# Routing in three batches of six tiles and one of seven, expert 0 split by ScalarE and VectorE, the gates' store before the expert loads

## The chip, the core and the metric

The program runs on one core of a Trainium2 chip. The metric is the device time of one execution in microseconds (us), lower is better. TensorE (PE) multiplies matrices out of SBUF into PSUM banks; VectorE (DVE), ScalarE (ACT) and GpSimd (POOL) work element by element; SyncE (SP) and the others issue transfers (DMA). Every engine runs its own list of instructions in order and waits for the others by semaphores.

## What is computed

A graph layer over 3125 nodes of 256 features and 53125 edges, sorted by the node they end at, and then a mixture of eight experts, of which each node uses its best two:

```python
h   = layernorm(x);  z = h @ W_func.T
e   = leaky_relu(concat(z[src], z[dst], edge_attr) @ W_att.T)
alpha = softmax of e over the edges of one dst
x   = x + h + relu(where(deg > 0, h @ W_self.T + segment_sum(alpha * z[src], dst), h))
t   = layernorm(x)                          # rows for the router and the experts
probs = softmax(t @ router_w.T);  top 2 of 8, renormalised -> gates
y_e = (silu(t @ w1[e].T) * (t @ w3[e].T)) @ w2[e].T
out = x + sum over e of gates[e] * y_e
```

## The kernel before

**The stream.** The nodes are 25 tiles of 128 rows (`TILES`); the edges are 104 groups of 512 (`GROUPS`). For each group POOL gathers four times 128 rows of z (`gather`, L826), DVE and ACT make the scores, their running maximum and the weights, PE multiplies them with the rows (`weighted`, L1347), and DVE adds the sums of two groups to `acc` (`add_sums`, L1869). `run` writes this as a software pipeline: in each turn a stage with lag n works on the group of n turns ago. The turns are 0 to 103 for group t's first stages, and go on until the stage with the largest lag is through. Stages passed through `tiled` work once in four turns on a node tile whose edges are complete: its denominator (`den_of`, L1581 to L1585), its share (ACT), a transpose and two products on PE (`node_parts`), the residual and second norm on DVE and ACT, the transpose and router product on PE (`hn2_T`, `logits_of`), and at the end `logit_copy` (L1626) with lag 34.

**Routing.** A batch of tiles (`ROUTES`) is routed on DVE once its logits are there: `first_choice`, `second_choice` (with the running counts `prefix`, L1673), `ranks_of` after two small products on PE (`rank_of`), `gates_of` (L1683 to L1690), and then pairs of one-hot rows for three tile and choice pairs at a time (`one_hots`, L1716 and L1717), which PE multiplies (`tokens_of`, L1277). The first three batches run in the stream, one step a turn behind the turn's other work; the last one after it, with the step that makes the list of slots (`slot_rows`, L1747) and of the expert of each slot.

**The experts.** There are 56 slots of 128 rows. Each expert's weights (`W`, 2.1 MB) are split into a high part (ACT copies it into the matrix type, L542) and a low part (the rest, a subtraction by `split_lo`, L551), in two pieces of 2842 and 1422 columns. Expert 0 is split by POOL alone (`split_first`, L558 and L563) once the stream's last product is done. Expert 1 is split by ACT and POOL while slot 0 runs (`second_hi`, `second_expert`). For the others ACT makes the high part, DVE the first low piece and POOL the second, in the turns after the expert's predecessor begins (`at_new_expert`). POOL gathers the rows of a slot (L876), PE transposes them, ACT and DVE make high and low rows (L1111, L1984), PE makes the first 384 hidden columns (`up_first`, L1411) and then the rest, ACT and DVE the gated hidden rows (L1118, L1970), PE transposes those (L1440), ACT and DVE split them (L1124, L1993, L1996), PE multiplies (L1450 for the high, L1457 for the low part), DVE weighs the result (`gated`, L2008, L2011) and POOL adds it into the output by an indirect transfer (L869).

**SP.** After the stream SP issues the loads of experts 1 and 2 (L696), then the gates' two stores (L770 for 20 tiles, L772 for 5), and then tells POOL that the first part is over. POOL's first gather of rows waits for both stores and for `slot_rows`. ACT's `second_hi` waits in turn 1 for expert 1's load, ahead of slot 0's first activation.

Of the kernel before, what the change touches and what calls it, by code (L numbers as in the profile page):

```python
# [30 lines left out]
P = 128  # L31
N, C, EDGES, EF = 3125, 256, 53125, 64
# [56 lines left out]
ROUTE_RING = 2  # L89
CHUNK = 3  # L90
# [13 lines left out]
def build(nc, x, src, src_batch, dst, dst_by_edge, dst_ends, mark_rows, wt, w_func, w_func_t, w_self_t, att_nodes, att_edge,  # L104
# [7 lines left out]
    with ExitStack() as ctx:  # L112
# [38 lines left out]
        split_next = sb("split_next", [1, SLOTS], i32)  # L151
# [4 lines left out]
        rt = sb("rt", [P, 4 * RB * E + 4 * RB * E + 5 * RB + (RB + 1) * E + 12 * RB + CELLS + TILES + 2 * E + 6 * E + 2  # L156
# [43 lines left out]
        iota_h, o = carve(ef, o, [2 * P], fp16)  # L200
        assert o <= 5 * WE
# [82 lines left out]
        gates, o = carve(rt, o, [TILES, E])  # L284
# [22 lines left out]
        split_f, o = carve(acc, o, [SLOTS])  # L307
        behind_f, o = carve(acc, o, [SLOTS])
        dump_p, o = carve(acc, o, [1])
# [96 lines left out]
        first_hi = sem("first_hi")  # L406
# [147 lines left out]
        def split_first(pool):  # L554
            pool.wait_ge(experts_in[0], 16)
            for piece in range(2):
                a, b = PIECES[piece]
                nc.gpsimd.tensor_tensor(split(0, 0, piece), raw(0, piece), ones[:, 0:1].to_broadcast([P, b - a]), ALU.mult)\  # L558
                    .then_inc(first_hi, 1)
            for piece in range(2):  # L560
                pool.wait_ge(first_hi, 1 + piece)
                pool.sem_inc(hi_split, 1)
                nc.gpsimd.tensor_tensor(split(0, 1, piece), raw(0, piece), split(0, 0, piece).bitcast(fp32), ALU.subtract)\  # L563
                    .then_inc(lo_split[piece], 1)

# [11 lines left out]
        def early_route(t):  # L577

            for b, (lo, hi) in enumerate(ROUTES[:-1]):
                i = t - BATCH * (hi - 1)  # L580
                if 0 <= i < 5 + CHUNKS_OF[b]:
                    return b, i
            return None, None

        def at_new_expert(eng, t, work):


            if isinstance(t, int) and t == 0:
                return
            e = eng.value_load(split_next[0:1, bass.ds(t, 1)], min_val=0, max_val=E - 1)  # L590
            with eng.If(e > 0):
                eng.wait_ge(y_psum, t)
# [1477 lines left out]
```

## Time and profile before

| | |
|---|---|
| median of 3 runs | 1061.29 us (1060.54 to 1061.91) |
| profiled execution | 1062.78 us, of which the span from first to last instruction is 1061.0 us |
| PE busy | 845.9 us (80%) |
| DVE busy | 648.2 us (61%) |
| POOL busy | 591.3 us (56%) |
| ACT busy | 449.6 us (42%) |
| last gather of the stream issued | 576.3 us |
| last product of the stream ends | about 604.7 us |
| routing of the last batch begins | 646.39 us |
| first expert product | 670.00 us |

The profiled execution is 1.49 us above the median of the runs, and 1.78 us of it lie outside the span. Times in the text are us from the start of the span. The program has three parts: up to 604.7 us the stream, up to 670 us a stretch of small dependent steps, and from there the 56 slots, in which PE is nearly always busy.

### The profile page before, as it was taken

The page shows a single profiled execution, that of the slowest core. Times are in us where ns is not written, and L with a number is a line of the kernel's source. Part 1 is how long each engine was busy: PE and PEld are TensorE (multiplying, and loading weights), DVE is VectorE, ACT ScalarE, POOL GpSimd, SP SyncE. Part 2 cuts the span into 40 slices and gives each one's busy share as a digit, 9 for nine tenths or more (in the row PEclk, how much of TensorE's full clock was granted, in tenths as well). Part 3 has the DMA queues.
Part 4 walks back from the last instruction along what each step waited for, and adds up shares of the span by engine and source line. Part 5 has one row for each costly group of instructions (what it writes and reads, how often), then busy time and mean ns, then how long its engine had stood idle before and what let it go on. Part 6 is the DMA issues. An engine that isn't in the chain of part 4 may idle for free. (4 is left out here: it accounts for less than half of the span.)

```text
span 1061.0 us, 18883 instructions
## 1 busy us (share of the span) xinstructions
PE 845.9 (80%) x4404; PEld 707.1 (67%) x4405; DVE 648.2 (61%) x2266; ACT 449.6 (42%) x1067; POOL 591.3 (56%) x558
## 2 busy tenths in 40 slices
PE   6955879866866667775688734799999999999995
PEld 6912445554655555664566633799999999999995
DVE  6634555655656696666676797356566565656553
ACT  4423243464465446556356811434344243443331
POOL 1177777777777777777775140634443544435332
PEclk9986989987888888898789956799999999999998
DMA  7776666565554455555454106442534422222221
GB/s 230 218 248 188 194 193 187 139 182 174 149 144 133 131 141 139 136 144 142 132 141 131 56 11 206 126 104 40 119 61 96 112 50 40 40 40 40 40 40 20
DMA packets 81157, 128.86 MB, mean 121 GB/s; under 512 B 21372, under 2 KB 56705, under 8 KB 80593
## 3 DMA queue, kind: packets, MB, share of 16 engines
q0 software_dynamic: 30720, 69.90, 28.2%
q1 hardware_dynamic: 43161, 51.59, 15.9%
q10 hardware_dynamic: 7200, 6.56, 1.8%
q8 instruction: 23, 0.38, 0.1%
q14 instruction: 53, 0.43, 0.1%
HBM read 106.86 MB, written 17.86 MB: 118 GB/s over the span
## 5 line engine op out<-in xcount | busy, mean ns | idle before, releaser
L826 POOL DMA_INDIRECT early<-ztab,early x416 | 398.1, 957 | 175.5 <-issue 172.8
L1347 PE MATMUL bank<-early,W 128*128 128x258 f32 x832 | 236.9, 438 | 14.3 <-DVE W L1846 11.5
L1411 PE MATMUL bank<-split_w,operands 128*128 x1344 | 237.6, 326 | 2.9 <-DVE operands L1984 1.4
L1411 PEld LDWEIGHTS bank<-split_w,operands 128*128 128x128 f32 x1344 | 213.4, 190 | 9.0 <-issue 6.7
L1347 PEld LDWEIGHTS bank<-early,W 128*128 128x128 f32 x832 | 174.2, 219 | 62.9 <-issue 30.9
L876 POOL DMA_INDIRECT xg<-ttab,slot_rows x56 | 55.5, 990 | 223.9 <-DVE late L2011 179.1
L1044 ACT ACTIVATE W<-early 128x128 f32<-128x128 f32 x208 | 91.0, 484 | 117.1 <-PE bank L1347 113.6
L1311 PE MATMUL bank<-ident,early 128*16 128x128 f32 x104 | 23.3, 368 | 128.2 <-DVE early L1829 128.2
L869 POOL DMA_INDIRECT out_rows<-late,slot_rows x56 | 88.9, 1588 | 32.8 <-issue 15.9
L1118 ACT ACTIVATE late<-bank 128x384 f32<-128x384 f32 x56 | 27.4, 490 | 183.8 <-PE bank L1411 183.7
L1311 PEld LDWEIGHTS bank<-ident,early 128*16 128x16 f32 x104 | 10.0, 117 | 140.2 <-DVE early L1829 137.8
L1450 PE MATMUL bank<-split_w,operands 128*128 x336 | 96.5, 395 | 1.5 <-ACT operands L1125 1.5
L1970 DVE TENSOR_TENSOR late<-late,bank 128x384 f32<-128x384 f32 x56 | 31.0, 554 | 73.0 <-ACT late L1118 73.0
L1033 ACT ACTIVATE early<-iota_row,W 128x128 f32<-128x128 f32 x208 | 70.6, 387 | 0.0
L1800 DVE TENSOR_TENSOR early<-edge_sb,early 128x4 f32<-128x4 f32 x104 | 16.3, 157 | 85.3 <-DMA early<-ztab,early 70.7
L2008 DVE TENSOR_SCALAR late<-bank,xg 128x256 f32<-128x256 f32 x56 | 27.1, 484 | 66.0 <-DMA out_rows<-late,slot_rows 43.6
L1450 PEld LDWEIGHTS bank<-split_w,operands 128*128 128x128 f32 x336 | 60.3, 188 | 9.6 <-issue 2.3
L1846 DVE TENSOR_SCALAR W<-iota_row,W,early 128x128 f32<-128x128 f32 x208 | 64.1, 360 | 0.4 <-ACT early L1026 0.4
L1869 DVE SCALAR_TENSOR_TENSOR acc<-bank,W,acc 128x258 f32 x104 | 45.8, 481 | 29.3 <-issue 17.6
L1202 PE MATMUL bank<-W,xg 128*32 128x512 f32 (+2 forms) x104 | 51.9, 631 | 7.8 <-DVE edge_sb L1574 4.1
L1993 DVE TENSOR_TENSOR operands<-bank,operands 128x512 fp32r<-128x512 f32 x112 | 49.7, 486 | 7.5 <-ACT operands L1124 3.6
L1020 ACT ACTIVATE early<-bank 128x32 f32<-128x32 f32 x26 | 5.1, 198 | 107.6 <-PE bank L1324 107.6
(230 smaller groups left out, 1428.4 us busy)
## 6 DMA issues: line engine op xcount, KB each, us to landing
W<-in_wt SPq DMA_DIRECT2D x26, 512.0 KB, 4.4
W<-in_experts SPq DMA_DIRECT2D x40, 266.5 KB, 2.8
early<-ztab,early POOLq DMA_INDIRECT x416, 3.0
W<-in_experts SPq DMA_DIRECT2D x3, 2132.0 KB, 8.7
early<-in_x SPq DMA_DIRECT2D x26, 128.0 KB, 2.1
early<-ztab SPq DMA_DIRECT2D x25, 128.0 KB
early<-late SPq DMA_DIRECT2D x25, 128.0 KB
out_rows<-early ACTq DMA_DIRECT2D x25, 128.0 KB, 1.9
```

Source lines behind the costliest of these rows:

```text
L826: nc.gpsimd.indirect_dma_start(out=zg[:, k * KG + c, :], out_offset=None, in_=ztab, in_offset=bass.IndirectOffsetOnAxis(ap=src_here[:, k / ...
L869: nc.gpsimd.indirect_dma_start(out=out, out_offset=bass.IndirectOffsetOnAxis(ap=slot_rows[:, 2 * t + 1:2 * t + 2], axis=0), in_=y_out[:, k ...
L876: nc.gpsimd.indirect_dma_start(out=xg[:, k, :], out_offset=None, in_=ttab, in_offset=bass.IndirectOffsetOnAxis(ap=slot_rows[:, 2 * t:2 * t ...
L1033: last = nc.scalar.activation(dist[:, k % 2, c * P:(c + 1) * P], iota_row[:, :], ACT.Abs, bias=dst_at[:, cols(t * KG + c, 1)], scale=-1.0)
L1044: last = nc.scalar.activation(prob_hot[:, k % 3, c * P:(c + 1) * P], dist[:, k % 2, c * P:(c + 1) * P], ACT.Relu, bias=prob[:, at:at + 1], ...
L1202: last = mm(ps[1][0:end - first, 0:G], att_pad[:, GROUPS - 2 - g:GROUPS - 2 - g + end - first], vec_in[:, n % W_RING, m * G:(m + 1) * G], ...
L1347: last = mm(ps[2 + k // 2 % 2][:, 0:ZR], prob_hot[:, k % 3, c * P:(c + 1) * P], zg[:, k * KG + c, :], start=(k % 2 == 0 and c == 0), stop= ...
L1411: last = mm(bank[:, 0:n], x[:, (k % 2 * KC + c) * P:(k % 2 * KC + c + 1) * P], split_w[:, bass.ds(at + (part + w + c * H), n)], start=(i = ...
L1450: return mm(ps[5][:, 0:2 * C].rearrange("p (b c) -> p b c", c=C), hidT_hi[:, i * P:(i + 1) * P], split_pairs[:, bass.ds(two, 2), W2_AT + i ...
L1846: last = v.tensor_scalar(prob_hot[:, k % 3, c * P:(c + 1) * P], iota_row[:, :], dst_at[:, cols(t * KG + c, 1)], prob[:, at:at + 1], ALU.is ...
L1869: v.scalar_tensor_tensor(acc[:, bass.ds(to, ZR)], ps[2 + k // 2 % 2][:, 0:ZR], of[:, cols(t - 1, 1)], acc[:, bass.ds(to, ZR)], ALU.mult, A ...
L1993: v.tensor_tensor(hidT_lo[:, at], bank[:, lo % 4 * P:lo % 4 * P + (hi - lo) * P], hidT_hi[:, at].bitcast(fp32), ALU.subtract)
```

## The change

- `ROUTES` becomes three batches of six tiles and a last one of seven. In the stream a batch's steps lie further apart: `prefix_of` has its own turn, `ranks_of` comes in the eighth (`rank_of` on PE in the seventh), the one-hot rows after it. The product for the ranks goes to bank 5 and no longer waits for node tiles.
- The last node tile is worked on three turns earlier in every stage (`LAST_AT`), with bank 0 for its router product.
- `split_first` is gone. ACT makes expert 0's high parts after the last batch's exponentials; DVE makes the first low piece when the slot list is done, and the second at the end of slot 0's `xT_low`.
- The table of where an expert is split is now three tables, computed in `split_turns`, on DVE behind the second low piece and ahead of slot 0's `hid_first`; expert lists with one or two slots are covered too. In DVE's turn `lo_piece` comes behind `gated` instead of before it.
- SP issues the gates' stores (18 and 7 tiles) before the loads of experts 1 and 2.

```diff
-ROUTES = ((0, 7), (7, 14), (14, 20), (20, TILES))
+ROUTES = ((0, 6), (6, 12), (12, 18), (18, TILES))
+LAST_AT = BATCH * (TILES - 2) + 1
...
             def at_group(t, k, r):
+                if t == LAST_AT:
+                    stage(TILES - 1, (TILES - 1) % NODE_RING, (TILES - 1) // NODE_RING)
                 j = r * NODE_RING + k // BATCH
-                if k % BATCH or (isinstance(j, int) and j >= TILES):
+                if k % BATCH or j >= TILES - 1:
                     return
...
-                sp.wait_ge(stream_over, 1)
+                gates_store()
                 for e in range(len(EXPERTS_AFTER), RAW):
                     expert_load(e)
...
-                pool.wait_ge(sums_psum, GROUPS)
-                split_first(pool)
...
                 exp_of(len(ROUTES) - 1)
+                act.wait_ge(experts_in[0], 16)
+                act.wait_ge(sums_psum, GROUPS)
+                split_hi(act, 0)
                 keep_tokens()
...
                     elif i == 2:
-                        ranks_of(b)
+                        prefix_of(b)
                     elif i == 3:
                         gates_of(b)
-                    elif b is not None and i < 4 + CHUNKS_OF[b]:
-                        one_hots(b, i - 4)
+                    elif i == 7:
+                        ranks_of(b)
+                    elif b is not None and 8 <= i < 8 + CHUNKS_OF[b]:
+                        one_hots(b, i - 8)
...
-            dve.wait_ge(expert_ready, 1)
+            split_lo(dve, v, 0, 0)
+
+            def split_turns():
+                split_lo(dve, v, 0, 1)
+                v.memset(changes, 0.0)
...
+                link(v.tensor_scalar(behind_f, exp_f, 1.0, None, ALU.add))
+                v.scalar_tensor_tensor(behind_f, exp_f, float(E - 1), behind_f, ALU.is_lt, ALU.mult)
+                link(v.tensor_tensor(changes[:, 1:SLOTS], exp_f[:, 1:SLOTS], exp_f[:, 0:SLOTS - 1], ALU.subtract))
+                link(v.tensor_tensor(after_all, changes[:, 0:SLOTS], behind_f, ALU.mult))
...
+                v.tensor_copy(split_both[0:1, :], for_dve[0:1, 0:SLOTS]).then_inc(expert_ready, 1)
+                dve.wait_ge(expert_ready, 2)
...
                 v.tensor_tensor(xT_lo[:, at], ps[4][:, 0:C], xT_hi[:, at].bitcast(fp32), ALU.subtract)\
                     .then_inc(xT_lo_ready, 1)
+                if isinstance(t, int) and t == 0:
+                    split_turns()
...
-            run(dve, SLOTS, RING, 1, [(1, hid_first), (2, hidT_low), (0, xT_low), (1, hid_second), (3, lo_piece),
-                                      (2, gated)])
+            run(dve, SLOTS, RING, 1, [(1, hid_first), (2, hidT_low), (0, xT_low), (1, hid_second), (2, gated),
+                                      (0, lo_piece)])
```

The first place is DVE's list around its last addition into `acc` (L1869 before, L1881 after), two turns into the stretch behind the last product. `rt` holds the routing's arrays. Before:

```order
L1665 COPY rt<-rt 128x8 [waits chain]
L1666 TENSOR_TENSOR rt<-rt 128x48
L1673 TENSOR_TENSOR rt<-rt 128x8 [waits choice_ready]
L1673 TENSOR_TENSOR rt<-rt 128x8 [waits chain] x5
L635 TENSOR_LOAD first_of
L635 ISA x2
L1869 ISA [waits next_added,sums_added,sums_psum]
...
L1699 TENSOR_TENSOR rt<-rt,bank6 128x96 [waits rank_psum]
L1702 TENSOR_REDUCE rt<-rt 128x12 [waits choice_ready]
L1703 CAST rt<-rt 128x12 [waits chain]
```

Now, at the same addition:

```order
L1732 TENSOR_SCALAR early<-early,rt 128x100
L1620 BN_STATS early<-early 128x6 [waits x2_ready]
L1625 BN_AGGR early<-early 128x2 [waits bn2_done]
L1731 TENSOR_SCALAR xg<-early,rt 128x256 [waits token_psum]
...
L635 TENSOR_LOAD first_of
L635 ISA x2
L1881 ISA [waits next_added,sums_added,sums_psum]
L1881 SCALAR_TENSOR_TENSOR acc<-bank3,W,acc 128x258
...
L1731 TENSOR_SCALAR xg<-early,rt 128x256 [waits token_psum]
L1732 TENSOR_SCALAR early<-early,rt 128x100
```

The third batch's choices, counts, gates and ranks now stand ahead of this place, in turns 102 to 109; two of its four one-hot steps (L1731, L1732) are still behind it.

The second place is DVE's list between slot 0's `xT_low` and its `hid_first`. Before, with the table's last steps ahead of it:

```order
L1756 TENSOR_TENSOR acc<-acc 128x55 [waits chain]
L1757 TENSOR_TENSOR acc<-acc 128x56 [waits chain]
L1758 CAST split_next<-acc 1x56 [waits chain]
L1759 MEMSET late 128x2x86
L606 UNCONDITIONAL_BRANCH
L1984 TENSOR_TENSOR operands<-bank4,operands 128x256 [waits xT_ready,expert_ready]
L1970 TENSOR_TENSOR late<-late,bank1 128x384 [waits silu_a]
```

Now:

```order
L561 TENSOR_TENSOR split_w<-W,split_w 128x2842 [waits lo_split0,hi_split]
L2022 TENSOR_TENSOR operands<-bank4,operands 128x256 [waits xT_ready]
L561 TENSOR_TENSOR split_w<-W,split_w 128x1422 [waits lo_split1,hi_split]
...
L1986 TENSOR_SCALAR acc<-acc 128x56
L1987 SCALAR_TENSOR_TENSOR acc<-acc 128x56 [waits chain]
L1988 TENSOR_TENSOR acc<-acc 128x55
...
L1999 TENSOR_TENSOR acc<-acc 128x56
L2000 TENSOR_TENSOR acc<-acc 128x56 [waits chain]
L2001 CAST split_act<-acc 1x56 [waits chain]
L2002 CAST slot_done<-acc 1x56
L2003 CAST split_both<-acc 1x56
L2008 TENSOR_TENSOR late<-late,bank1 128x384 [waits silu_a,expert_ready]
```

Between `xT_low` (now L2022) and `hid_first` (now L2008) stand a low piece, four memsets and 18 small operations on arrays in SBUF; nothing stood there before.

The third place is the end of a DVE turn with a low piece, in the loop over the slots. Before:

```order
L1977 TENSOR_TENSOR late<-late,bank3 128x298
L590 REGISTER_ALU
L590 TENSOR_LOAD split_next
L590 ISA x2
L591 COMPARE_AND_BRANCH
...
L551 TENSOR_TENSOR split_w<-W,split_w 128x2842
...
L2008 TENSOR_SCALAR late<-bank5,xg 128x256
L2011 SCALAR_TENSOR_TENSOR late<-bank5,xg,late 128x256 [waits y_half]
L1970 TENSOR_TENSOR late<-late,bank1 128x384 [waits silu_a]
```

Now:

```order
L2015 TENSOR_TENSOR late<-late,bank3 128x298
...
L2050 TENSOR_SCALAR late<-bank5,xg 128x256
L2053 SCALAR_TENSOR_TENSOR late<-bank5,xg,late 128x256 [waits y_half]
...
L585 TENSOR_LOAD split_both
L585 ISA x2
L586 COMPARE_AND_BRANCH
...
L561 TENSOR_TENSOR split_w<-W,split_w 128x2842
L586 UNCONDITIONAL_BRANCH
L2008 TENSOR_TENSOR late<-late,bank1 128x384 [waits silu_a]
```

The low piece (L551, now L561), with the table look-up and the branch ahead of it, moved from before `gated` to directly before the next turn's `hid_first`.

## Rows read from the trace of the kernel before

**Rows 1.** Windows: busy PE, PEld, DVE, ACT, POOL; PE's clock, DMA share, GB/s.

```profile
577.00:604.80 27.80, 26.88 (x141) 22.84 (x140) 19.24 (x77) 24.86 (x59) 0.22 (x1) 1.00 0.27 79
604.80:621.50 16.70, 0.36 (x4) 0.12 (x2) 16.53 (x7) 2.29 (x5) 16.69 (x4) 0.67 0.00 1
621.50:646.40 24.90, 17.31 (x72) 13.92 (x72) 17.34 (x87) 8.04 (x18) 0.00 (x1) 0.71 0.11 38
```

**Rows 2.** Costliest groups: the stream's gathers; busy, mean ns, idle before.

```profile
L826 POOL DMA_INDIRECT early<-ztab,early x416 | 398.1, 957 | 175.5 <-issue 172.8
```

**Rows 3.** Timeline behind the stream's last product: start, us, engine, line, operation.

```profile
604.81 7.44 POOL L558 TENSOR_TENSOR split_w<-W,ones 128x2842 fp32r<-128x2842 f32 x2 [27.59 <-PE bank L1347]
604.96 4.84 DVE L1644 TENSOR_TENSOR rt<-rt 128x48 f32<-128x48 f32 x1
609.83 2.48 DVE L1645 TENSOR_TENSOR rt<-rt 128x48 f32<-128x48 f32 x1
612.21 9.30 POOL L563 TENSOR_TENSOR split_w<-W,split_w 128x2842 fp32r<-128x2842 f32 x2
612.35 0.20 DVE L1646 TENSOR_REDUCE rt<-rt 128x6 f32<-128x48 f32 x1
612.58 5.85 DVE L1647 TENSOR_TENSOR rt<-rt 128x48 f32<-128x48 f32 x1
618.47 3.06 DVE L1665 COPY rt<-rt 128x8 f32<-128x8 f32 x1
```

**Rows 4.** Timeline from there on, DVE: counts, ranks, gates, one-hots, last tile.

```profile
621.68 1.17 DVE L1673 TENSOR_TENSOR rt<-rt 128x8 f32<-128x8 f32 x6
...
624.61 0.25 DVE L1702 TENSOR_REDUCE rt<-rt 128x12 f32<-128x96 f32 x1
...
626.65 0.20 DVE L1683 TENSOR_REDUCE rt<-rt 128x6 f32<-128x48 f32 x1
...
629.63 0.28 DVE L1716 TENSOR_SCALAR xg<-early,rt 128x256 f16<-128x256 f16 x1
...
630.04 0.28 DVE L1716 TENSOR_SCALAR xg<-early,rt 128x256 f16<-128x256 f16 x1
...
633.99 0.15 DVE L1581 TENSOR_SCALAR has_edge<-acc 128x1 f32<-128x1 f32 x1
```

**Rows 5.** The same timeline, the last write of the slot list.

```profile
661.31 0.21 DVE L1747 TENSOR_TENSOR slot_rows<-acc 128x56 int32<-128x56 f32 x1
```

**Rows 6.** The chain that ended last, into POOL's first gather of rows.

```profile
652.29 11.42 DMA ttab<-rt
...
663.74 0.75 issue
```

**Rows 7.** Timeline of slots 0 and 1.

```profile
668.95 3.84 ACT L542 ACTIVATE split_w<-W 128x2842 fp32r<-128x2842 f32 x2
669.15 0.42 DVE L1984 TENSOR_TENSOR operands<-bank,operands 128x256 fp32r<-128x256 f32 x1 [5.08 <-ACT operands L1111]
...
670.00 4.20 PE L1411 MATMUL bank<-split_w,operands 128*128 x12 [1.45 <-DVE operands L1984]
671.59 9.51 POOL L551 TENSOR_TENSOR split_w<-W,split_w 128x2842 fp32r<-128x2842 f32 x2 [2.36 <-ACT split_w L542]
...
674.76 0.56 DVE L1970 TENSOR_TENSOR late<-late,bank 128x384 f32<-128x384 f32 x1 [5.18 <-ACT late L1118]
...
683.15 2.26 PE L1411 MATMUL bank<-split_w,operands 128*128 x12
```

**Rows 8.** Timeline of a turn with a low piece (expert 2's).

```profile
730.19 3.12 DVE L551 TENSOR_TENSOR split_w<-W,split_w  x1 [0.91 <-PE bank L1450]
733.22 0.48 DVE L2008 TENSOR_SCALAR late<-bank,xg 128x256 f32<-128x256 f32 x1
...
735.50 0.29 DVE L1996 TENSOR_TENSOR operands<-bank,operands 64x128 fp32r<-64x128 f32 x1
735.84 0.65 PEld L1457 LDWEIGHTS bank<-split_w,operands 128*128 128x128 f32 x5 [0.27 <-DVE operands L1996]
```

More of the change, by code:

```diff
@@ L200, in build @@
         iota_h, o = carve(ef, o, [2 * P], fp16)
+        gates, o = carve(ef, o, [TILES, E])
         assert o <= 5 * WE
@@ L306, in build @@
         exp_f, o = carve(acc, o, [SLOTS])
-        split_f, o = carve(acc, o, [SLOTS])
         behind_f, o = carve(acc, o, [SLOTS])
+        changes, o = carve(acc, o, [SLOTS + 2])
+        after_all, o = carve(acc, o, [SLOTS])
+        after_1, o = carve(acc, o, [SLOTS])
+        after_2, o = carve(acc, o, [SLOTS])
+        after_3, o = carve(acc, o, [SLOTS])
+        longer, o = carve(acc, o, [SLOTS])
+        for_act, o = carve(acc, o, [SLOTS + 3])
+        for_dve, o = carve(acc, o, [SLOTS + 3])
+        for_done, o = carve(acc, o, [SLOTS + 3])
         dump_p, o = carve(acc, o, [1])
@@ L552, in split_lo @@
                 .then_inc(lo_split[piece], 1)
[L554 to L564, printed above, removed]
         def chunk_no(b, i):
@@ L982, in hn2T_copy @@
                     act.wait_ge(logit_psum, j)
-                nc.scalar.activation(hn2T, ps[7][:, 0:C], ACT.Copy).then_inc(hn2T_ready, 1)
+                nc.scalar.activation(hn2T, router_bank(j)[:, 0:C], ACT.Copy).then_inc(hn2T_ready, 1)
             def x2_store(j, k, r):
@@ L1229, in node_parts @@
                     pe.wait_ge(or_idle, j)
-                for b, (lo, hi) in enumerate(ROUTES[:-1]):
-                    if in_stream and j == hi + 2:
-                        pe.wait_ge(choice_ready, 3 * b + 3)
                 for c in range(KC):
@@ L1264, in rank_of @@
                 pe.wait_ge(choice_ready, 3 * b + 1)
-                pe.wait_ge(or_idle, min(hi + 2, TILES))
-                mm(ps[6][:, C:C + n * E], before[:, :], both[:, 0:n * E], start=True, stop=False)
+                mm(ps[5][:, RANK_AT:RANK_AT + n * E], before[:, :], both[:, 0:n * E], start=True, stop=False)
                 pe.wait_ge(choice_ready, 3 * b + 2)
-                last = mm(ps[6][:, C:C + n * E], ones[:, 0:P], prefix[:, 0:n * E], start=False, stop=True)
+                last = mm(ps[5][:, RANK_AT:RANK_AT + n * E], ones[:, 0:P], prefix[:, 0:n * E], start=False, stop=True)
                 if b == len(ROUTES) - 1:
-                    last = mm(ps[6][:, C + RB * E:C + (RB + 1) * E], ones[:, 0:P], prefix[:, n * E:(n + 1) * E],
+                    last = mm(ps[5][:, RANK_AT + RB * E:RANK_AT + (RB + 1) * E], ones[:, 0:P], prefix[:, n * E:(n + 1) * E],
                               start=True, stop=True)
@@ L1331, in mirror_back @@
                     pe.wait_ge(back_ready, batch(k, r) + 1)
+                    for b, (lo, hi) in enumerate(ROUTES[:-1]):
+                        if batch(k, r) == hi + 8:
+                            pe.wait_ge(choice_ready, 3 * b + 3)
                     mm(ps[5][:, 0:BC], mirror[:, :], back_sb[:, BC:2 * BC], start=True, stop=True).then_inc(mirrored, 1)
@@ L1421, in up_first @@
                 pe.wait_ge(xT_lo_ready, t + 1)
-                for piece in range(2):
-                    pe.wait_ge(lo_split[piece], e + 1)
+                pe.wait_ge(lo_split[0], e + 1)
                 if at_least(t, 1):
+                    pe.wait_ge(lo_split[1], e + 1)
                     pe.wait_ge(hid_a_ready, t)
@@ L1999, in lo_piece @@
             def lo_piece(t, k, r):
[L2000 removed]
+                if isinstance(t, int) and t < 2:
+                    return
+                split_named(dve, split_both, t, lambda e: split_lo(dve, v, e, 0))
             def gated(t, k, r):
```

113 lines of the change are left out of this document (68 added, 45 removed).

## The prediction

> **What bounds the kernel now.** I read the busy windows first, then the groups, then the timeline from the stream's end on, because the change leaves most of the 1061 us alone. In the stream POOL paces itself: 416 gathers of 957 ns, with 175.5 us of idle time of which 172.8 us are its own issue gaps [rows 2], so it waits for nobody until its last gather at 576 us. Work that the change puts into the stream's turns before that lies under it. From 577 to 604.8 us, when the gathers are in, PE is the bound, busy 26.88 of 27.8 us at full clock, and DVE has 27.8 - 19.24 = 8.6 us to spare [rows 1]. Then comes a stretch of 65 us with PE mostly idle. Its first 16.7 us are a surprise: PE works 0.36 us, and DVE is "busy" 16.53 us with seven operations [rows 1]. The timeline shows why: from 604.81 us on POOL splits expert 0, and each DVE operation with two inputs in SBUF, and the copy, ends only when the POOL instruction under way ends. 48 columns take 4.84, 2.48 and 5.85 us, the 8-column copy 3.06 us; the reduction between them, with one input, takes 0.20 us [rows 3]. After 621.5 us the chain is DVE's small operations and the last tiles' steps, to 646.4 us; then the last batch's routing, and POOL's gather, held by the gates' second store: 11.42 us long behind the two expert loads, then 0.75 us to the gather's start [rows 6]. From 670 us on PE sets the pace, and anything that makes it wait once is lost.
>
> **The change part by part.** The profiled execution took 1062.78 us, 1.49 above the median; the terms are differences taken from its timeline, and I put their sum on the median of 1061.29.
>
> *The split on POOL goes.* The four held operations took 4.84 + 2.48 + 5.85 + 3.06 = 16.2 us; at 0.2 us each, as the unheld one, they take 0.8 [rows 3]. **-15.4 us.** Here a rule of the Trainium skill fits: SBUF, State Buffer, section "Who interferes with whom", says that a VectorE operation with two SBUF inputs and a GpSimd one that reads SBUF take turns at a shared pair of ports, held for a whole instruction by whoever came first. By this trace it holds, reduction and all [rows 3]; it speaks for this term and against the one on `split_turns` below, and neither sum needs it.
>
> *Work leaves the stretch.* The third batch had its counts (1.17 us), ranks (seven operations of about 0.19 us, 1.3), gates (eight of 0.2 to 0.24, 1.8) and four steps of one-hots after 604.8 us. A pair of one-hots is issued every 0.41 us (630.04 - 629.63), so a step of three takes 1.25 us [rows 4]. All but two of these steps move into turns 102 to 111: 1.17 + 1.3 + 1.8 + 2.5 = **-6.8 us**.
>
> *It arrives in the PE-bound stretch.* Added to DVE before the last product: both choices (3.0 us together, of which about 2 stood there already), 1.2, 1.8, 1.3 and 2.5, some 7.8 us, against 8.6 us of idle time [rows 1]. On average it fits; by turns it doesn't. DVE's turns 103 to 105 carry 1.6, 1.2 and 1.8 us more where a turn of PE lasts about 3 us, and PE needs DVE's weights of the turn before. Following the turns I get 2.7 us by turn 107 and another 1.2 at turns 109 and 110, for ranks and one-hots. **+3.7 us**; bounds 0 (all idle time is used) and 7.8 (none is).
>
> *The last tile three turns earlier.* Its denominator came at 633.99 us behind two one-hot steps [rows 4]; now it follows the tile before it at once, and its transpose waits for no router copy. The two chains share ACT and PE, so most of the head start is lost: **-1.5 us**, bounds 0 and -4.
>
> So the last batch's routing should begin 15.4 + 6.8 - 3.7 + 1.5 = 20.0 us earlier, near 626.4 us.
>
> *The last batch, seven tiles for five.* Four more pairs of one-hots (1.7 us), two more chained counts (0.4), wider operations (0.2): +2.3 us to the slot list. Before, that list stood at 661.52 us, 2.2 us before the gates' landing at 663.74 [rows 5, 6]. With the stores first the gates no longer end last, and the gather starts 0.75 us behind the list. **+0.1 us.** The loads now start some 7 us into this batch's routing. Before, both loads and both stores were through the queue 17.3 us after the loads' issue (646.4 to 663.7), so even that long they end about 24 us in, and slot 0's first product came 23.6 us in (670.00 - 646.4) [rows 1, 6, 7]. Expert 1, first in the queue, is needed about then and has half the bytes. I take nothing; bound +3.
>
> *Expert 0 on ACT and DVE.* ACT's 3.84 us for two high pieces [rows 7] lie under 10 us in which ACT waits for the one-hot products. DVE's first low piece, 3.12 us [rows 8], starts 1.6 us behind the list and ends 4.7 us behind it; `xT_low` came 5.4 us behind the gather's release (669.15 - 663.74) [rows 6, 7]. It is just hidden; should the cover shrink, each us costs one.
>
> *`split_turns`.* This is the place where a stall comes back. It stands between `xT_low` and `hid_first` of slot 0. DVE was idle there for 5.18 us [rows 7]; a low piece of half the columns (1.6 us) and 18 small operations (about 3 us) would fit, were DVE alone. But at 671.59 us POOL starts to split expert 1, 9.51 us long, and it will do so again, since it is released by ACT's first high piece. DVE ends `xT_low` at 669.57, the low piece at about 671.2, memsets and one scalar operation at 671.6. What follows are two-input operations and copies in SBUF, of the kinds held before. One ends when POOL's first piece ends, one when the second does, at 681.1; the other 15 take 2.4 us. `hid_first` then runs at about 683.6 instead of 674.76 us [rows 7], and `xT_low` of slot 1 behind it at 684.1 to 684.5. PE, which went straight into slot 1's first products at about 676.6 us (24 products in a row), begins them at 684.8: +8.2 us. PE has then stood still for 8 us. In the stretch from 604.8 us, idle all through, its granted clock averages 0.67 [rows 1], so it had fallen from 2.4 to 1.2 GHz within the first 6 us or so. The first 12 products of a slot take 4.20 us at 1.2 GHz against 2.26 at 2.4 [rows 7]: +1.9 us. **+10.1 us**; bounds 0 (nothing is held) and 12 (POOL's instructions stretch too).
>
> *`lo_piece` behind `gated`.* In the turns with a low piece PE already waits for DVE: the weights of the low product were loaded 0.27 us late, released by L1996 [rows 8]. DVE took the low piece at 730.19 to 733.31, while PE finished the slot, and `gated` after it. Now `gated` must wait for that slot's end (about 730.3) and takes 1.0 us, then come look-up and branch, and the piece starts at about 731.9 and ends at 735.0; before, the next turn started at 734.14. That is 0.9 us later, and PE waits 0.9 us longer, once for each of the six experts 2 to 7. **+5.4 us**; bounds 0 and 6 x 1.7 = 10.
>
> Sum: -20.0 + 0.1 + 10.1 + 5.4 = -4.4 us, so **1057 us**.
>
> **The rivals.**
> 1. *DVE isn't held in `split_turns`* (15%). It would be so if these operations slipped in between POOL's, or were through before it. Against it: four of four such operations were held under the same POOL instruction [rows 3]. Then the 10.1 us go: 1061.3 - 14.5 = 1046.8 us.
> 2. *The turn order costs nothing* (15%): the wait for `gated` lies where DVE idles anyway, and look-up and branch overlap. Against it is the 0.27 us wait of PE [rows 8]; for it, that the gap ahead of the low piece was 0.91 us and may hide a wait of another kind. Then 1061.3 - 9.8 = 1051.5 us.
> 3. *Slower* (10%): the low piece, now directly ahead of `hid_first`, delays it by its whole 3.12 us in each of the six turns, because `gated` ends only when the hidden rows are already there. 6 x 3.12 = 18.7 us in place of 5.4: 1061.3 - 4.4 + 13.3 = 1070 us. It decides the sign from (4.4 + 5.4) / 6 = 1.6 us a turn on.
>
> My forecast has 60%; its own range is 1052 to 1062 us, from the stream's delay (0 to 7.8) and the turns (0 to 10) that don't go wrong together.
>
> **How the numbers follow.** The range must leave out no more than 2 in 10: below, 1046 cuts half of the first rival (7%); above, 1063 cuts the third (10%) and a little of my own case (2%). A difference within 0.2% (2.1 us) can't be told from none here. My own case is faster than that 77 times in 100, the same 21, slower 2; rivals 1 and 2 are faster, 3 slower. Together: faster 0.76, same 0.13, slower 0.11.
>
> **What the profile after would show.** Right: no DVE operation over 1 us behind the last product; the last batch's first reduction near 626 us; the second gates' store landing before the slot list; in slot 0 two small DVE operations of some 6 and 3 us under POOL's low pieces and PE idle for 8 us, with a halved clock behind it; six turns in which the low product's weights wait about 1 us for DVE. Wrong, if the stream's last product ends much later than 609 us, if DVE's small operations in slot 0 stay at 0.2 us, or if the slots' period at an expert's change doesn't move.

## The result, and the profile after

The changed kernel is slower: 1071.62 us median of 4 runs (1070.39 to 1072.54) against 1061.60 for the kernel before in the same comparison, a ratio of 1.0093 (95% interval 1.0076 to 1.0111). The forecast of 1057 and its range to 1063 both missed. The profiled execution has a span of 1069.3 us where the one before had 1061.0. Of all the executions compared below, one of e3 took 2001.73 us where its six others took 1055.6 to 1061.4 us; its ratio leaves that one out.

One event divides the span well: the write of the slot list, from which POOL's gathers of rows start. It was over at 661.52 us before [rows 5] and is over at 645.30 now, 16.2 us earlier. From there to the end it was 399.5 us and is now 424.0, 24.5 us more. The first part went nearly as forecast in its sum, the second didn't.

Windows of the profile after, the stretches behind the stream's gathers (columns as in [rows 1]):

```profile
577.00:604.80 27.80, 24.06 (x119) 20.27 (x117) 21.24 (x92) 19.50 (x50) 0.00 (x0) 0.94 0.21 59
604.80:621.50 16.70, 12.89 (x49) 9.96 (x47) 8.94 (x40) 4.07 (x11) 0.00 (x0) 0.69 0.10 32
621.50:646.40 24.90, 9.46 (x38) 6.41 (x38) 18.77 (x97) 8.31 (x12) 0.27 (x1) 0.56 0.49 186
```

Against [rows 1] PE works 12.89 us instead of 0.36 in the 16.7 us in which POOL held DVE. The stream's last product ended at 603.75 us (604.72 before), and the last router result is there at 627.48 (646.19 before). The gathers were done sooner: POOL issued the last one at 570.5 us instead of 576.3, most of it because its issue gaps between them fell to 167.8 us in all, from 172.8 [rows 2]:

```profile
L829 POOL DMA_INDIRECT early<-ztab,early x416 | 397.4, 955 | 170.6 <-issue 167.8
```

Nothing in the forecast has this. It isn't the missing split on POOL that does it (e6 and e8 below lack the split too and have gaps as before); which of the other edits it is, no run shows.

The timeline from the last router result to the slot list, and the first slot:

```profile
627.48 0.17 DVE L1638 COPY logits<-bank 128x8 f32<-128x8 f32 x1 [1.39 <-PE bank L1257]
...
645.09 0.21 DVE L1763 TENSOR_TENSOR slot_rows<-acc 128x56 int32<-128x56 f32 x1
...
646.13 0.94 POOL L875 DMA_INDIRECT xg<-ttab,slot_rows  x1 [74.64 <-DVE slot_rows L1763]
...
646.57 0.20 DVE L1769 MEMSET late<- 128x172 f32 x1
...
649.91 3.12 DVE L561 TENSOR_TENSOR split_w<-W,split_w 128x2842 fp32r<-128x2842 f32 x1 [3.14 <-issue]
650.58 0.38 ACT L1121 ACTIVATE operands<-bank 128x256 fp32r<-128x256 f32 x1 [7.50 <-PE bank L1159]
650.86 3.84 ACT L552 ACTIVATE split_w<-W 128x2842 fp32r<-128x2842 f32 x2
652.95 0.41 DVE L2022 TENSOR_TENSOR operands<-bank,operands 128x256 fp32r<-128x256 f32 x1
...
653.51 10.66 POOL L561 TENSOR_TENSOR split_w<-W,split_w 128x2842 fp32r<-128x2842 f32 x2 [2.68 <-ACT split_w L552]
...
655.11 5.98 DVE L1986 TENSOR_SCALAR acc<-acc 128x56 f32<-128x56 f32 x1
...
661.12 3.13 DVE L1987 SCALAR_TENSOR_TENSOR acc<-acc 128x56 f32<-128x56 f32 x1
664.17 0.20 DVE L1988 TENSOR_TENSOR acc<-acc 128x55 f32<-128x55 f32 x1
...
667.13 0.56 DVE L2008 TENSOR_TENSOR late<-late,bank 128x384 f32<-128x384 f32 x1
...
668.41 4.13 PE L1421 MATMUL bank<-split_w,operands 128*128 x12 [8.17 <-DVE operands L2022]
```

The gather starts right behind the list: the stores no longer end last (the last gates' store is issued at 634.33 us and lands in 2.1 us). The first low piece waits 3.14 us for nothing that the profile shows, and `xT_low` waits for the piece, 2.0 us longer than for ACT's copy (650.96). Of the table's operations two are held by POOL's pieces of expert 1, 5.98 and 3.13 us, and the third takes 0.20 again. PE stands still for 8.17 us.

The second loss is at the changes of expert. The timeline of the first one:

```profile
714.93 0.42 ACT L1141 ACTIVATE late<-bank 128x298 f32<-128x298 f32 x1 [0.73 <-PE bank L1421]
...
716.97 3.86 ACT L552 ACTIVATE split_w<-W  x2 [1.62 <-PE bank L1462]
...
723.39 0.46 DVE L2015 TENSOR_TENSOR late<-late,bank 128x298 f32<-128x298 f32 x1
...
724.67 0.49 DVE L2050 TENSOR_SCALAR late<-bank,xg 128x256 f32<-128x256 f32 x1 [0.82 <-PE bank L1462]
725.20 0.48 DVE L2053 SCALAR_TENSOR_TENSOR late<-bank,xg,late 128x256 f32<-128x256 f32 x1
...
726.77 3.12 DVE L561 TENSOR_TENSOR split_w<-W,split_w  x1 [1.09 <-issue]
727.25 4.11 POOL L868 DMA_INDIRECT out_rows<-late,slot_rows  x1 [0.30 <-issue]
...
729.80 0.55 DVE L2008 TENSOR_TENSOR late<-late,bank 128x384 f32<-128x384 f32 x1
...
731.51 0.65 PEld L1469 LDWEIGHTS bank<-split_w,operands 128*128 128x128 f32 x5 [1.60 <-DVE operands L2036]
```

The low piece starts 2.9 us after `hid_second` ends (723.85), behind `gated` (which waits 0.82 us for PE and takes 1.0) and then 1.09 us of look-up and branch; before it was 0.9 us (729.28 to 730.19). Over the six changes it starts 2.7 to 2.9 us behind `hid_second`, where it was 0.2 to 0.9, and in all six `hid_first` starts on the piece's end. PE's low weights come 1.60 us late, where it was 0.27 [rows 8]. ACT's high pieces start 1.62 us behind its last activation (0.64 before). Measured between successive `hid_first`, a usual slot takes 6.62 us; the two that see a high and a low piece took 7.34 and 7.48 before and take 8.33 and 8.57 now. From `hid_first` of slot 7 to that of slot 44, with all six changes between them, it was 250.6 us and is 265.3: 14.7 us more.

### The profile page after: what moved, and what is told of

Its sections match the earlier page's. It is cut to its first block and busy times, and to the rows that moved or that the text cites. A ratio compares the mean times of both kernels' runs of the same rounds, so it can differ in the third digit from the quotient of the medians.

```text
span 1069.3 us, 18908 instructions
## 1 busy us (share of the span) xinstructions
PE 850.3 (80%) x4404; PEld 707.4 (66%) x4405; DVE 648.9 (61%) x2284; ACT 449.9 (42%) x1067; POOL 589.0 (55%) x554
## 5 line engine op out<-in xcount | busy, mean ns | idle before, releaser
L829 POOL DMA_INDIRECT early<-ztab,early x416 | 397.4, 955 | 170.6 <-issue 167.8
L1421 PE MATMUL bank<-split_w,operands 128*128 x1344 | 240.9, 329 | 14.3 <-DVE operands L2022 11.4
L868 POOL DMA_INDIRECT out_rows<-late,slot_rows x56 | 103.3, 1845 | 32.6 <-issue 16.0
L1462 PE MATMUL bank<-split_w,operands 128*128 x336 | 96.9, 396 | 4.8 <-ACT operands L1135 4.8
L2008 DVE TENSOR_TENSOR late<-late,bank 128x384 f32<-128x384 f32 x56 | 31.1, 555 | 91.1 <-ACT late L1128 91.1
L1812 DVE TENSOR_TENSOR early<-edge_sb,early 128x4 f32<-128x4 f32 x104 | 16.7, 161 | 91.1 <-DMA early<-ztab,early 78.2
L1881 DVE SCALAR_TENSOR_TENSOR acc<-bank,W,acc 128x258 f32 x104 | 45.9, 482 | 31.6 <-issue 17.9
```

What stands on the lines that cost most here:

```text
L829: nc.gpsimd.indirect_dma_start(out=zg[:, k * KG + c, :], out_offset=None, in_=ztab, in_offset=bass.IndirectOffsetOnAxis(ap=src_here[:, k / ...
L868: nc.gpsimd.indirect_dma_start(out=out, out_offset=bass.IndirectOffsetOnAxis(ap=slot_rows[:, 2 * t + 1:2 * t + 2], axis=0), in_=y_out[:, k ...
L1421: last = mm(bank[:, 0:n], x[:, (k % 2 * KC + c) * P:(k % 2 * KC + c + 1) * P], split_w[:, bass.ds(at + (part + w + c * H), n)], start=(i = ...
L1462: return mm(ps[5][:, 0:2 * C].rearrange("p (b c) -> p b c", c=C), hidT_hi[:, i * P:(i + 1) * P], split_pairs[:, bass.ds(two, 2), W2_AT + i ...
L1881: v.scalar_tensor_tensor(acc[:, bass.ds(to, ZR)], ps[2 + k // 2 % 2][:, 0:ZR], of[:, cols(t - 1, 1)], acc[:, bass.ds(to, ZR)], ALU.mult, A ...
```

## The experiments

All ratios are to the kernel before, timed on the same chip. The columns behind them are read from each run's profile: the span, the time at which the slot list is written, from there to the end, and from slot 7's `hid_first` to slot 44's.

| kernel | ratio (95% interval) | span | list | list to end | slots 7 to 44 |
|---|---|---|---|---|---|
| before | 1 | 1061.0 | 661.5 | 399.5 | 250.6 |
| changed | 1.0093 (1.0076 to 1.0111) | 1069.3 | 645.3 | 424.0 | 265.3 |
| e1, POOL behind tables | 0.9968 (0.9951 to 0.9985) | 1061.0 | 647.4 | 413.6 | 265.3 |
| e2, one look-up on ACT | 1.0038 (1.0022 to 1.0055) | 1063.8 | 644.9 | 418.9 | 260.2 |
| e3, low piece ahead of gated | 0.9960 (0.9942 to 0.9978) | 1056.6 | 645.1 | 411.6 | 252.7 |
| e4, e1 to e3 together | 0.9856 (0.9833 to 0.9880) | 1043.0 | 642.6 | 400.4 | 251.5 |
| e5, piece in the branch | 1.0056 (1.0034 to 1.0078) | 1066.7 | 643.7 | 423.0 | 265.1 |
| e6, before, split off POOL | 0.9887 (0.9870 to 0.9903) | 1051.3 | 647.8 | 403.5 | 250.8 |
| e7, before, stores first | 1.0004 (0.9991 to 1.0017) | 1062.7 | 661.8 | 400.9 | 251.3 |
| e8, e6 and e7 | 0.9843 (0.9820 to 0.9865) | 1048.0 | 647.9 | 400.1 | 250.5 |
| e9, e4 and e5 | 0.9843 (0.9824 to 0.9862) | 1039.3 | 639.6 | 399.7 | 251.3 |
| e10, changed, turns of before | 0.9865 (0.9846 to 0.9884) | 1047.5 | 644.3 | 403.2 | 251.1 |
| e11, e10 and e5 | 0.9838 (0.9822 to 0.9855) | 1044.3 | 644.5 | 399.8 | 251.2 |

The same stream ended between 601.8 and 607.8 us in the nine kernels that have it as changed, so single spans differ by a few us that no edit made; the two columns on the right don't hold that scatter.

### e1: POOL splits expert 1 behind the tables

```diff
                 if isinstance(t, int) and t == RING - 1:
+                    pool.wait_ge(expert_ready, 2)
                     for piece in range(2):
```

> The changed kernel with one wait more: POOL starts the low pieces of expert 1 only when DVE has written the tables of the turns. Theory A (POOL's two low pieces hold the table operations, 5.98 and 3.13 us for two of them): these two take 0.2 us each, hid_first of slot 0 runs at about 658.5 us instead of 667.13, PE's stop of 8.17 us goes and with it the halved clock behind it: 1071.6 - 8.2 - 1.9 = about 1061.5 us. Theory B (18 small operations and their links need that long by themselves, or DVE waits for something else there): no change, 1071.6 us. In between, near 1067, if POOL's pieces, moved behind the tables, hold DVE in slots 1 and 2 instead.

DVE and POOL in slot 0 of this run:

```profile
657.21 0.12 DVE L1987 TENSOR_SCALAR acc<-acc 128x56 f32<-128x56 f32 x1
657.36 0.22 DVE L1988 SCALAR_TENSOR_TENSOR acc<-acc 128x56 f32<-128x56 f32 x1
...
660.52 9.55 POOL L561 TENSOR_TENSOR split_w<-W,split_w 128x2842 fp32r<-128x2842 f32 x2 [7.60 <-DVE split_both L2004]
660.63 0.56 DVE L2009 TENSOR_TENSOR late<-late,bank 128x384 f32<-128x384 f32 x1 [0.20 <-ACT late L1129]
```

Theory A holds. The two held operations take 0.12 and 0.22 us, the 18 take 3.2 us together, and `hid_first` waits for ACT, not for DVE. From the list to the end it is 10.4 us less, by the edit of one wait; POOL's pieces, moved behind, hold nobody: `hid_first` at 660.63 takes its usual 0.56 us under them. That this is because one of its two inputs lies in PSUM is likely, but no run varies it. The timed gain, 1.0093 - 0.9968 or 13 us, is larger than the 8.3 us between the spans; the intervals of the two ratios together leave about 2.5 us either way, and I take the profile's 10.4.

### e2: ACT's second look-up

```diff
-                    act.wait_ge(y_psum, act.value_load(slot_done[0:1, bass.ds(t, 1)], min_val=1, max_val=SLOTS))
+                    if at_least(t, 4):
+                        act.wait_ge(y_psum, t - 3)
```

The wait that is left is enough for experts with several slots, as all have here; one with a single slot would need the table.

> The changed kernel with ACT's second table look-up taken out of the turns with a high piece: it waits for the product of four slots ago, computed from the turn's number, instead of for the slot that the table slot_done names. Theory A (the second look-up makes ACT's high pieces start 1.0 us later than before, and silu_first behind them, and hid_first, and PE with them): the gap ahead of the high pieces falls from 1.36 to 1.66 us to 0.6 to 1.2 us, the slot's period in these six turns from 8.3 to about 7.3 us, time 1071.6 - 6 x 1.0 = about 1065.6 us. Theory B (the low piece on DVE, one turn later, sets the pair's loss, and PE catches up): under 2 us less, 1070 us or more.

ACT's timeline at the first change of expert:

```profile
714.60 0.42 ACT L1142 ACTIVATE late<-bank 128x298 f32<-128x298 f32 x1 [0.73 <-PE bank L1422]
715.97 3.86 ACT L552 ACTIVATE split_w<-W  x2 [0.94 <-issue]
```

The gap ahead of the high pieces falls from 1.36 to 1.66 us to 0.76 to 1.12 in the six turns, and their slots take 7.4 to 7.8 us instead of 8.1 to 8.3 (the first 7.65). Slots 7 to 44 are 5.1 us shorter. In the changed kernel 1.4 of those us are something else: at the third change PE's twelve products took 3.74 us instead of 2.3, as the granted clock fell to 1.2 GHz just there, after PE had waited 0.98 and 0.58 us. It did so in one other run (e5); e1 lost the same 1.5 us at its first change instead. So the look-up is worth 0.6 us a change. Most of the loss stays, and it isn't ACT's.

### e3: the low piece ahead of `gated`

```diff
-            run(dve, SLOTS, RING, 1, [(1, hid_first), (2, hidT_low), (0, xT_low), (1, hid_second), (2, gated),
-                                      (0, lo_piece)])
+            run(dve, SLOTS, RING, 1, [(1, hid_first), (2, hidT_low), (0, xT_low), (1, hid_second), (0, lo_piece),
+                                      (2, gated)])
```

> The changed kernel with one entry moved: in DVE's turn the low piece stands ahead of gated again. Theory A (in the changed kernel the low piece starts 1.8 us later in its turn, 1.0 for gated and 1.1 for look-up and branch that no longer lie under the wait for the slot's product; PE gets 1.1 us of it, six times): six periods of 8.4 fall to about 7.4 us, time 1071.6 - 6 x 1.1 = 1065 us. Theory B (the 3.12 us of the piece cost the same wherever they stand): within 1.5 us of 1071.6.

DVE's timeline at the first change of expert:

```profile
722.39 0.46 DVE L2015 TENSOR_TENSOR late<-late,bank 128x298 f32<-128x298 f32 x1
723.03 3.12 DVE L561 TENSOR_TENSOR split_w<-W,split_w  x1 [0.17 <-issue]
726.06 0.48 DVE L2050 TENSOR_SCALAR late<-bank,xg 128x256 f32<-128x256 f32 x1
```

Theory A in kind, and twice its size: 12.6 us in slots 7 to 44, 2.1 a change (1.4 us of the whole again the clock). The piece starts 0.17 us behind `hid_second` instead of 2.9, since `gated` and its wait for PE no longer stand between them. The idle time directly ahead of the piece is 0.14 to 0.34 us in the six turns, where it was 0.91 to 1.09 behind `gated`. It isn't always so short in this order: in e4 and e9, with the same operations running ahead of it, it is 0.14 to 0.91 us, and no run shows on what that depends. The first pair of slots takes 8.02 + 6.75 = 14.77 us against 14.82 in the kernel before and 16.90 in the changed one, though ACT's second look-up is still there. Over all six changes e3 is still 2.1 us behind the kernel before (252.7 for 250.6).

### e4: the three together

> The changed kernel with the edits of the three runs before together: POOL's pieces of expert 1 behind the tables, ACT's second look-up out, the low piece ahead of gated. The spans gave 8.3, 5.5 and 12.7 us apart. Theory A (three separate delays in three separate turns, so they add up): span near 1043 us, time near 1045. Theory B (high piece and low piece delay the same pair of turns, so that what one gives back the other takes): the 5.5 us of the look-up are lost again, about 1050 us.

From the list to the end 400.4 us, 23.6 us less than in the changed kernel, and within 0.9 us of the kernel before. By the totals theory A looks right (span 1043.0, expected 1043), but slots 7 to 44 take 251.5 us, only 1.2 less than with e3 alone: of e2's 5.1 us most is lost, as theory B says, and the span agrees because the list came 2.7 us earlier in this execution. The profiled execution was the fastest of the four, whose median of 1047.75 us lies between the theories. So ACT's second look-up costs 3.8 us where the low piece is late as well, and 1.2 where it isn't.

### e5: the first low piece inside the branch

```diff
                 route_rest(len(ROUTES) - 1)
+                split_lo(dve, v, 0, 0)
...
-            split_lo(dve, v, 0, 0)
```

> The changed kernel with DVE's first low piece of expert 0 moved into the branch, directly behind the slot list and ahead of the jump out of it. In the changed kernel the piece starts at 649.91 us, 3.14 us after the last operation in the branch, and xT_low waits for its end at 653.03 although ACT's copy for it is there at 650.96. Theory A (the 3.14 us are the way out of the branch, and pass while nothing else is to do): the piece runs at 646.8 to 649.9, the way out takes as long behind it, xT_low runs at 653.0, no gain: 1071.6 us. Theory B (the 3.14 us run from the jump's own time, or shrink while the piece runs, since DVE's queue goes on while the piece is under way): xT_low at about 651.0, 2.0 us gained, 1069.6 us. In both, POOL's second to fourth gather of rows, issued while the piece runs, take up to 3 us longer.

DVE, POOL and ACT behind the slot list:

```profile
644.53 0.95 POOL L875 DMA_INDIRECT xg<-ttab,slot_rows  x1 [71.54 <-DVE slot_rows L1763]
...
645.10 3.04 DVE L561 TENSOR_TENSOR split_w<-W,split_w 128x2842 fp32r<-128x2842 f32 x1
645.78 3.18 POOL L875 DMA_INDIRECT xg<-ttab,slot_rows  x1 [0.30 <-issue]
...
648.96 0.38 ACT L1121 ACTIVATE operands<-bank 128x256 fp32r<-128x256 f32 x1 [7.48 <-PE bank L1159]
...
649.38 0.42 DVE L2022 TENSOR_TENSOR operands<-bank,operands 128x256 fp32r<-128x256 f32 x1 [1.23 <-ACT operands L1121]
```

Theory B: DVE's way out of the branch passes while the piece runs, and `xT_low` waits for ACT alone. Slot 0's first product stands 6.4 us behind the list instead of 8.4. Only 1.0 of these 2.0 us reaches the end (423.0 for 424.0), since the tables behind it are held until POOL's pieces end. What those 3.1 us are no run here takes apart; some 3 us stood ahead of DVE's first operation outside the branch in e1 (3.13), e2 (3.34), e3 (2.81), e4 (3.09) and e10 (2.81) too. The Trainium skill (Runtime: NRT & Kernel Launch, "Instruction fetch mechanics") says that a taken branch to code outside the window held makes the engine fetch it before it goes on; by this rule the gap is a fetch. The trace is in keeping with it: between 646.4 and 650.0 us the changed kernel has four packets of the kind `instruction`, of 77 in the whole span. It doesn't show for which engine they are.

### e6, e7, e8: parts of the change on the kernel before

e6 takes `split_first` out of POOL, and has:

```diff
+                act.wait_ge(experts_in[0], 16)
+                act.wait_ge(sums_psum, GROUPS)
+                split_hi(act, 0)
                 keep_tokens()
...
                 route_rest(len(ROUTES) - 1)
+                for piece in range(2):
+                    split_lo(dve, v, 0, piece)
```

> The kernel before with one part of the change alone: ACT takes expert 0's high pieces behind the last exponentials, DVE both low pieces behind the slot list, and POOL's split is gone; batches, tables, turns and stores are those of before. Theory A (the four held operations cost 15.4 us, all on the path): no DVE operation over 1 us behind the last product, the slot list 15.4 us earlier; the two low pieces and whatever follows them delay xT_low by about 3 us: 1061.6 - 15.4 + 3 = 1049 us. Theory B (the held stretch hid other work, such as the last tiles' products and stores): less than 10 us gained, 1052 us or more.

e7 has only the stores moved:

```diff
                 sp.wait_ge(stream_over, 1)
+                gates_store()
                 for e in range(len(EXPERTS_AFTER), RAW):
                     expert_load(e)
```

> The kernel before with one part of the change alone: both stores of the gates ahead of the two expert loads in SP's queue. Theory A (the second store, 11.42 us behind the loads, is what held the gather, 2.2 us behind the slot list): the gather starts at about 662.3 instead of 664.49 us, 1061.6 - 2.1 = 1059.5 us. Theory B (the loads, 6 us later, come too late for expert 1 or for the gather's own transfers, which now share the DMA engines with them): no gain or a loss, 1061.6 us or more.

> The kernel before with two parts of the change: expert 0 split on ACT and DVE, and the gates' stores first; turns, tables and batches are those of before. In the run with the split alone the gather waited for the second store, 11.40 us behind the loads, and POOL's first gather took 4.96 us, because DVE's two low pieces were under way. With the stores first it is released 0.75 us behind the slot list, before the pieces start, and takes 0.95 us. Theory A: the first product of slot 0 then waits for DVE (pieces to 654.9, then the way out of the branch, 3 us) and comes at about 658.7 instead of 660.21 us: 1.5 us less than that run, about 1050 us. Theory B (DVE's way out of the branch passes under the pieces): first product near 656.5, about 1048 us.

In e6 the distance from the stream's last product to the list is 41.4 us, for 56.8 before: 15.4 us gone, the whole of the four held operations. From the list to the end it takes 4.0 us more, and the time falls by 12 us (0.9887; the spans, by 9.7, with the stream's end 1.7 us later in this execution). The 4.0 us are seen in its chain and on POOL:

```profile
638.58 11.40 DMA ttab<-rt
650.01 0.75 issue
650.76 7.20 DMA xg<-ttab,slot_rows
```

```profile
650.31 4.59 DVE L550 TENSOR_TENSOR split_w<-W,split_w 128x2842 fp32r<-128x2842 f32 x2
...
650.76 4.96 POOL L859 DMA_INDIRECT xg<-ttab,slot_rows  x1 [71.42 <-DMA ttab<-rt]
656.02 0.94 POOL L859 DMA_INDIRECT xg<-ttab,slot_rows  x1 [0.30 <-issue]
```

The store stands behind the loads as before, and the gather starts 2.9 us behind the list as before (3.0). What is new is that POOL's gather, issued while DVE subtracts, takes 4.96 us in place of 0.99, so that slot 0's first product stands 12.4 us behind the list instead of 8.5. Theory A had the 15.4 us right and about the size of what is given back, 3 us, but not its way: `xT_low` waits for the gathered rows, not for the pieces. In e7, the stores moved alone, theory B holds. The gather starts 1.8 us earlier, but its transfer takes 1.7 us longer, and the loads now run beside it: the queue of the loads (q1) moves 1.02 MB in these 4.97 us, where it moved 0.27 MB in the 3.26 us before. Another 0.8 us pass between `xT_low` and the first product. First the chain of the kernel before, then that of e7:

```profile
664.49 3.26 DMA xg<-ttab,slot_rows
```

```profile
662.65 4.97 DMA xg<-ttab,slot_rows
```

Together (e8) they are worth more than apart: the list comes 13.6 us earlier than before, the first gather is not held (the third is, for 4.56 us, with nobody waiting for it), the first product is at 656.78, and from the list to the end it is 400.1 us. Theory A expected 658.7 for that product, theory B 656.5; this is B, as in e5. That is the simplest of the fast kernels, with two parts of the change and none of the others.

### e9, e10, e11: what the tables and turns are worth

e10 is the changed kernel with one table, written in the branch, and the lags of the kernel before. Its core:

```diff
-            run(dve, SLOTS, RING, 1, [(1, hid_first), (2, hidT_low), (0, xT_low), (1, hid_second), (2, gated),
-                                      (0, lo_piece)])
+            run(dve, SLOTS, RING, 1, [(1, hid_first), (2, hidT_low), (0, xT_low), (1, hid_second), (3, lo_piece),
+                                      (2, gated)])
```

> The changed kernel with four edits: POOL's pieces of expert 1 behind the tables, ACT's second look-up out, the low piece ahead of gated, and DVE's first low piece of expert 0 inside the branch. Theory A (the piece in the branch brings its 2.6 us here too): span 1043.0 - 2.6 = 1040.4 us. Theory B (with POOL out of the way, DVE's chain of second piece and tables ends just as ACT's silu_first of slot 0 does, so xT_low may come earlier but hid_first can't): under 1 us gained, span 1042 to 1043 us.

> The changed kernel without its part on the turns: one table, written in the branch, ACT's and DVE's pieces three turns behind as before, the low piece ahead of gated; batches, stores, the last tile's place and expert 0 on ACT and DVE stay. Theory A (both losses, in slot 0 and at the six changes of expert, come from that part alone): six table operations stand ahead of the first low piece (1.2 us), slot 0's first product at about 654.9 us, and from there to the end as long as in the kernel before with its split taken off POOL and the stores first (391.2 us): span 1046 us, about 1047 us timed, 2 us less than that kernel. Theory B (the batches and the last tile's place give nothing beyond what the executions scatter by): span 1048 us, the same as that kernel.

> The same with DVE's first low piece of expert 0 inside the branch. Theory A (as in the run with that edit alone, 2.6 us): span about 1043.5 us. Theory B (the six table operations ahead of it use up the cover, since POOL's second gather is held by the piece and the way out of the branch comes behind it): under 1 us gained.

e10 takes 251.1 us from slot 7 to 44 and 403.2 from the list to the end: without the part on the turns 20.8 of the 24.5 us are gone. The span, 1047.5 us, lies nearer to theory B's 1048 than to A's 1046, and its reason is A's missing term. With no tables to compute there was still something for POOL to hold, the second low piece itself:

```profile
652.89 6.29 POOL L551 TENSOR_TENSOR split_w<-W,split_w 128x2842 fp32r<-128x2842 f32 x1 [3.12 <-DVE split_w L551]
652.99 7.69 DVE L551 TENSOR_TENSOR split_w<-W,split_w 128x1422 fp32r<-128x1422 f32 x1
```

It started 0.1 us after POOL's and took 7.69 us. In e11 it is through before POOL begins (650.56 us, 1.63 long), and 3.4 us are back: list to end 399.8 for 403.2. This is theory A: the medians differ by its 2.6 us, the spans by 3.1. In e9 theory B holds: 0.7 us gained (399.7 for 400.4); its span of 1039.3 is low because the stream ended at 601.8 us in that execution. e8, e9 and e11 are 1.6% faster than the kernel before, with intervals that overlap each other's.

## Why the prediction was wrong

**What held.** *The split on POOL goes*, -15.4: measured 15.4 between last product and list (e6). *Seven tiles for five*, +2.3: from the last router result to the list it is 17.8 us in all nine kernels with the changed stream and 15.3 to 15.4 in the four without, +2.5. The list was forecast for 643.8 and came at 645.3. The gather follows it by 0.83 us (0.75 forecast). *`split_turns`*, +10.1: between slot 0's first product (16.3 us earlier than before) and slot 1's `hid_first` (6.25 earlier) 10.1 us went, in the two operations named, with PE idle for 8.2; and e1 takes 10.4 away.

**Right by luck.** The list's time is a sum in which terms missed in opposite directions. Means of the nine kernels with the changed stream, against e6 and e8, which have the stream of before and no split on POOL: the last gather comes at 571.4 us for 578.5, -7.1, which no term had; from there to the stream's last product it is 32.8 us for 28.0, +4.9, where *it arrives in the PE-bound stretch* had +3.7; from there to the last router result 22.1 for 26.1, -4.0, where *work leaves the stretch* and *the last tile three turns earlier* had -8.3 together. With the +2.5 this is -3.7, where the forecast's terms give -2.3. So half of the gain claimed behind the last product isn't there, and the earlier gathers made up for it. Single executions scatter by up to 5 us in the gathers' end and 4 us in the last distance, so the halves are rough, the signs are not.

**Expert 0 at nothing.** This was 2.0 us. I had the piece start 1.6 us behind the list; it started 4.6 behind, because DVE needed 3.1 us from the last operation in the branch to the first outside. The kernel before has the same branch to leave there, but DVE waited 5.08 us for ACT anyway [rows 7], so its trace doesn't show what the way out took.

**`lo_piece` behind `gated`**, +5.4. This is the step that failed: 14.7 us instead of 5.4. Taken apart by the runs, the late piece with ACT as before costs 9.5 us (e2, 260.2 - 250.6), 1.6 a change where I had 0.9; ACT's second look-up on top of it 3.8 (0.6 a change); the clock 1.4. I had the delay of the piece somewhat short (1.7 us; it was 2.0 in the turn that I read, 2.2 on average of the six), and took 0.8 of it for slack, read from one turn of the trace; the 1.6 us that reach the end leave 0.6. And ACT's new look-up stood in no term at all, though the diff shows it; I had costed ACT's edits only in slot 0.

The third rival, slower at 1070 us by 3.12 us in each of six turns, came nearest in its time. By its own bound, 1.6 us a turn, the sign turned: 14.7 / 6 = 2.4. Its mechanism is in the trace, in a smaller size: `hid_first` starts on the piece's end in all six turns, 2.0 to 2.6 us after ACT's output for it is there, where it was 0.7 to 1.2 before. But its slot is longer than a usual one by 1.95 us at the first change and not by 3.12, and half of what was lost there lay in the turn before, with ACT's high piece. The first two rivals, a DVE that isn't held and a turn order that costs nothing, are refuted by e1 and e3.

The sum of what was measured: -16.2 (list) - 0.1 (the gather 2.1 us sooner behind the list, the piece 2.0) + 10.1 + 14.7 = +8.5 us, where the spans differ by 8.3. Of the 12.9 us between this and the forecast of -4.4, `lo_piece` is 9.3, expert 0 is 2.0 and the list 1.5.

## What to carry to other kernels

When an instruction with a table look-up and a branch is moved, ask what stands just ahead of it: behind an instruction that waits for another engine it cost 0.91 to 1.09 us in every turn, and the work that it guards waited as well; behind operations under way it cost 0.14 to 0.91. A stall removed in one place (here POOL's split against DVE) comes back wherever small operations are put beside the same partner; one wait that orders the two (e1) cost nothing and gave 10 us. And a change of many parts should be timed by parts: with two of this one's alone (e8) the time was as low as with any other set that ran.

## What the runs showed of the hardware

- POOL and DVE hold each other both ways. A subtraction with two inputs in SBUF on DVE made POOL's gather take 4.96 us (e6), 3.18 (e5) and 4.56 (e8) instead of 0.95, each ending 0.8 us behind the end of the DVE operation. At the changes of expert six of POOL's 56 additions into the output took 3.9 to 4.1 us instead of 1.6, beside DVE's low piece. The Trainium skill (SBUF — State Buffer, "Who interferes with whom") has such a DVE operation contend with a GpSimd instruction that reads SBUF. These transfers take their row numbers from `slot_rows` in SBUF, so the rows are in keeping with it.
- Which of the two comes first decides by tenths of a us: the same 1422 columns took 7.69 us started 0.1 us behind POOL's piece (e10), 1.62 us started 0.2 us ahead of it (the changed kernel, 653.29 and 653.51 us).
- DVE's way out of a branch took 2.8 to 3.3 us in the six kernels in which it stood idle there, and was covered when a 3 us operation was the last inside (e5).
- The granted clock fell once to 1.2 GHz in the middle of the slots, where PE had waited 0.98 and 0.58 us in one turn; this cost 1.4 us. In e5 it fell at the same place, in e1 at another change, and in e2, with the same waits, not at all.
